# Graph attention with turned scores and a graph convolution with tiles of one bin each, in a new order of operations

## What is computed

```python
# graph attention (edges sorted by dst)
el = jnp.sum(feat_src_e * attn_l[edge_type], axis=-1)
er = jnp.sum(feat_dst_e * attn_r[edge_type], axis=-1)
e = jax.nn.leaky_relu(el + er, negative_slope=0.2)
m = jax.ops.segment_max(e, edge_dst, num_segments=N_NODES)
ex = jnp.exp(e - m[edge_dst])
denom = jax.ops.segment_sum(ex, edge_dst, num_segments=N_NODES)
h = jax.ops.segment_sum((ex / denom[edge_dst])[..., None] * feat_src_e, edge_dst, num_segments=N_NODES)
# graph convolution
filt = jax.nn.silu(rbf @ Wf1 + bf1) @ Wf2 + bf2
agg = jax.ops.segment_sum(x[col] * filt, row, num_segments=N_NODES)
```

## Time and profile before

| | |
|---|---|
| median of 3 runs | 4170.98 us (4170.66 to 4171.43) |
| the profiled execution | 4176.44 us |
| its span, first to last instruction | 4174.7 us |
| PE busy | 2928.3 us, 70% of the span |
| DVE busy | 2177.3 us, 52% |
| ACT busy | 1210.5 us, 29% |
| POOL busy | 2277.2 us, 55% |
| mean granted TensorE clock | 0.858 of full speed |

### The profile page before, as it was taken

One profiled execution on the slowest core, in us unless ns is written; L12 is line 12 of the kernel. 1 busy time (PEld: TensorE's weight loads), 2 busy tenths in 40 slices (PEclk: granted clock), 3 DMA queues, 4 the chain that ended last, 5 costly groups with the idle time before them and its releaser, 6 DMA issues. The chain is left out here.

```text
span 4174.7 us, 73619 instructions
## 1 busy us (share of the span) xinstructions
PE 2928.3 (70%) x20296; PEld 2364.7 (57%) x20297; DVE 2177.3 (52%) x5961; ACT 1210.5 (29%) x3266; POOL 2277.2 (55%) x2336
## 2 busy tenths in 40 slices
PE   5199101777777777776379679999999864299990
PEld 1188101555555555555255358888888633288990
DVE  8411002877777777777743557777777444011112
ACT  1123000444444444444223223333333231022220
POOL 2777775777777777777240056666666200511115
PEclk8599655998998999999679789999999875599995
DMA  3344101222222222225100143333335501155533
GB/s 105 108 135 137 40 2 32 63 65 63 63 64 63 64 64 63 64 64 62 23 19 1 47 136 89 90 89 90 90 90 84 52 0 39 49 175 173 171 104 114
DMA packets 209214, 317.71 MB, mean 76 GB/s; under 512 B 63367, under 2 KB 150063, under 8 KB 208388
## 3 DMA queue, kind: packets, MB, share of 16 engines
q0 software_dynamic: 95008, 179.89, 19.9%
q1 hardware_dynamic: 103204, 127.24, 9.4%
q10 hardware_dynamic: 10944, 9.97, 0.7%
HBM read 248.03 MB, written 68.84 MB: 76 GB/s over the span
## 5 line engine op out<-in xcount | busy, mean ns | idle before, releaser
L1402 POOL DMA_INDIRECT conv_got<-xtab,conv_rowidx x588 | 565.8, 962 | 313.2 <-DVE conv_msg L1507 156.6
L806 POOL DMA_INDIRECT att_got<-feat,att_rowidx x588 | 573.2, 975 | 201.5 <-issue 150.2
L294 POOL DMA_INDIRECT table<-l0a_rec,l0a_addr x469 | 458.2, 977 | 216.7 <-issue 146.1
L1454 PE MATMUL conv_pf<-conv_wf,conv_act 128*128 128x256 f32 x2352 | 534.0, 380 | 0.2 <-DVE conv_filt L1502 0.2
L812 POOL DMA_INDIRECT table<-recs_rec,recs_addr x432 | 423.2, 980 | 131.6 <-issue 130.4
L1454 PEld LDWEIGHTS conv_pf<-conv_wf,conv_act 128*128 128x128 f32 x2352 | 447.6, 190 | 76.9 <-issue 0.8
L982 PE MATMUL att_pmax<-all_identb,att_away 128*128 128x512 bf16 x588 | 261.1, 444 | 203.9 <-DVE att_elo L901 203.2
L863 DVE TENSOR_REDUCE att_tmax<-att_pmax 128x4 f32<-128x512 f32 x588 | 373.8, 680 | 31.1 <-PE att_pmax L986 27.6
L986 PE MATMUL att_pmax<-all_identb,att_ehi 128*128 128x128 bf16 x2352 | 383.6, 242 | 0.0
L986 PE MATMUL att_pmax<-all_identb,att_elo 128*128 128x128 bf16 x2352 | 383.3, 242 | 0.0
L1420 ACT ACTIVATE conv_act<-conv_p,conv_bf 128x512 f32<-128x512 f32 x294 | 186.2, 684 | 552.1 <-PE conv_p L1446 552.1
(11 more groups left out here) (336 smaller groups left out, 5074.0 us busy)
## 6 DMA issues: line engine op xcount, KB each, us to landing
moe_w<-in_L_ffn_w SPq DMA_DIRECT2D x96, 512.0 KB
feat<-proj_out SPq DMA_DIRECT2D x30, 1040.0 KB
results<-moe_y ACTq DMA_DIRECT2D x76, 128.0 KB, 1.7
att_got<-feat,att_rowidx POOLq DMA_INDIRECT x588
conv_got<-xtab,conv_rowidx POOLq DMA_INDIRECT x588, 2.8
xtab<-ln_row SPq DMA_DIRECT2D x60, 128.0 KB, 1.7
table<-l0a_rec,l0a_addr POOLq DMA_INDIRECT x469
table<-recs_rec,recs_addr POOLq DMA_INDIRECT x469, 2.1
```

Source lines behind the costliest of these rows:

```text
L294: self.nc.gpsimd.indirect_dma_start(out=self.table, out_offset=bass.IndirectOffsetOnAxis(ap=self.addrs[:, j:j + 1], axis=0), in_=self.recs ...
L806: nc.gpsimd.indirect_dma_start(out=got[g % 3][:, k, :], out_offset=None, in_=feat, in_offset=bass.IndirectOffsetOnAxis(ap=rowidx[:, g * K ...
L1402: nc.gpsimd.indirect_dma_start(out=got[g % 3][:, k, :], out_offset=None, in_=xtab, in_offset=bass.IndirectOffsetOnAxis(ap=rowidx[:, g * K ...
L1454: ins = nc.tensor.matmul(pf[b][:, k, :], act1[s3][:, h, (2 * b + k) * P:(2 * b + k + 1) * P], wf2[:, h, :], start=(h == 0), stop=(h == 1))
```

## The change

The convolution gets its own padding: `table1` is sorted into tiles of one bin each instead of groups of one bin, so it needs ET1 = 500 tiles, or 125 groups of four. The four tiles of a group can now belong to four bins: TensorE writes four sums, two to a bank, VectorE loads four bin numbers and makes four additions to `agg`, spread over the step between other work.

In attention the scores of a group are written as bf16 parts into `spread`, turned by TensorE (`pE`), copied by ScalarE (`eT`) and brought into `pmax` by one matmul of 512 columns a tile, which a constant `select` directs; so `pmax` takes eight matmuls of 512 columns a group. VectorE reduces all four banks in one instruction. ScalarE scales `acc` by `keep` (`shrunk`, four instructions), and VectorE adds `psum` in one. The pipeline has four slots and five stages (groups t to t-4), the kinds of all edges (`typ`) are computed once ahead of the loop, and the order in each engine's step is new: sums, products and additions of old groups stand early in a step, and small dependent instructions alternate with others.

The sends to `table1` are redistributed: 214 in attention (none for the first four groups, then one or two in turn), 12 beside `join_attention`, 26 beside the second layer norm, 24 beside the mixture's routing, 167 in the mixture and 26 beside the third layer norm. The numbers of all sends and of the gathers in attention stay.

The diff, cut; for the steps of `attend`, whose old form stands above, only the new side is shown.

```diff
 K = 4
 ET = 588
 TS = ET + -(-EJ // P)
+ET1 = 500
+TS1 = ET1 + -(-EJ // P)
+assert (EDGES + NT * (P - 1)) // P <= ET1 and ET1 % K == 0
 assert 0 < EV <= EJ and (EDGES + NT * (K * P - 1)) // (K * P) <= ET // K and ET % (3 * K) == 0
 COLS0 = 20, 44, EJ - 64
-ROUND = 3
-COLS1 = ROUND * (ET // K - 3), EJ - ROUND * (ET // K - 3)
-assert sum(COLS0) == EJ == sum(COLS1) and COLS1[1] > 0
+COLS1 = ET // K - 4 + (ET // K - 4) // 2, 12, 26, 24, 167, 26
+assert sum(COLS0) == EJ == sum(COLS1)
 RELS, HEADS, HD = 8, 4, 64
 FW = D + HEADS
 NG = 20
...
+            sends = [0 if g < SLOTS else 1 + g % 2 for g in range(GROUPS)]
+            assert sum(sends) == COLS1[0]
             for g in range(GROUPS):
+                u = g % SLOTS
                 if g >= SLOTS:
+                    pool.wait_ge(f_ready, g - SLOTS + 1)
+                    pool.wait_ge(last_ready, (g - SLOTS + 1) * LAST)
                 for k in range(K):
                     nc.gpsimd.indirect_dma_start(
...
+                wait_positive(pool, sent[u], 16 * sum(sends[u:g:SLOTS]))
+                for i in range(sum(sends[:g]), sum(sends[:g + 1])):
                     nc.gpsimd.indirect_dma_start(
                         out=table1, out_offset=bass.IndirectOffsetOnAxis(ap=addr1[:, i:i + 1], axis=0),
+                        in_=rec1[:, i, :], in_offset=None).then_inc(sent[u], 16)
+            for u in four:
+                pool.wait_ge(sent[u], 16 * sum(sends[u::SLOTS]))
...
+            v.memset(acc[:, :, :, :], 0.0).then_inc(ready, 1)
...
+            v.tensor_tensor(typ[:, :, :], bcast(c["ramp"][:, 0:RELS], [[0, ET], [1, RELS]]),
+                            recs[:, :, 2].unsqueeze(2).broadcast_to([P, ET, RELS]), ALU.is_equal).then_inc(ready, 1)
...
+                    at = [bcast(spread[s1][:, 0, q * K * HEADS:], [[HEADS, K], [ROWS + 1, HEADS]]) for q in range(2)]
+                    dve.wait_ge(er_ready, g1 + 1)
+                    v.tensor_tensor(ert[:, :, :, :], per[:, :, 0:RELS * HEADS].rearrange("p k (r h) -> p k h r", r=RELS),
+                                    typ[:, bass.ds(g1 * K, K), :].unsqueeze(2).broadcast_to([P, K, HEADS, RELS]), ALU.mult).then_inc(picked, 1)
+                    dve.wait_ge(picked, g1 + 1)
+                    v.tensor_reduce(ers[:, :, :], ert[:, :, :, :], AX.X, ALU.add).then_inc(ers_ready, 1)
                 if 0 in parts:
...
+                    wait_positive(dve, sum_ready, t - 3)
...
+                if 1 in parts:
+                    dve.wait_ge(got_s[s1], ((i + 1) if u else i) * 16 * K)
+                    dve.wait_ge(ers_ready, g1 + 1)
+                    v.tensor_tensor(z[:, :, :], ers[:, :, :], got[s1][:, :, D:FW], ALU.add).then_inc(z_ready, 1)
...
+                    dve.wait_ge(ex_ready, g3 + 1)
+                    wait_positive(dve, sum_ready, g3 - 1)
+                    n = ON_DVE
+                    v.tensor_tensor(f[(u - 3) % 2][:, 0:n, :, 0:HD], got[s3][:, 0:n, 0:D].rearrange("p k (h d) -> p k h d", h=HEADS),
+                                    ex[:, 0:n, :].unsqueeze(3).broadcast_to([P, n, HEADS, HD]), ALU.mult).then_inc(f_ready, 1)
+                if 4 in parts:
+                    bin4 = bin_of(dve, g4)
+                if 1 in parts:
+                    dve.wait_ge(z_ready, g1 + 1)
+                    v.scalar_tensor_tensor(out=e[s1][:, :, :], in0=z[:, :, :], scalar=SLOPE, in1=z[:, :, :], op0=ALU.mult, op1=ALU.max).then_inc(e_done, 1)
+                if 4 in parts:
+                    dve.wait_ge(sum_ready, g4 + 1)
...
+                    dve.wait_ge(sum_ready, g4 + 1)
+                    dve.wait_ge(shrunk_ready, (g4 + 1) * HEADS)
+                    v.tensor_tensor(flat(flat(acc[:, bass.ds(bin4, 1), :, :], "p a b c -> p a (b c)")), flat(shrunk[:, :, :]), psum[:, 0:HEADS * H1], ALU.add).then_inc(acc_done, 1)
+                if 1 in parts:
+                    dve.wait_ge(e_done, g1 + 1)
+                    wait_positive(dve, spread_turned, g1 - 3)
+                    v.tensor_copy(at[0], e[s1][:, :, :]).then_inc(high, 1)
...
+                    dve.wait_ge(max_ready, g2 + 1)
+                    v.tensor_reduce(tmax[:, :], pmax[:, :, :, :].rearrange("p k h e -> p h k e"), AX.XY, ALU.max).then_inc(tmax_ready, 1)
+                    bin2 = bin_of(dve, g2)
+                if 1 in parts:
+                    dve.wait_ge(high, g1 + 1)
+                    v.tensor_tensor(at[1], e[s1][:, :, :], at[0], ALU.subtract).then_inc(e_ready, 1)
+                if 2 in parts:
+                    m = flat(mrun[:, bass.ds(bin2, 1), :])
+                    dve.wait_ge(tmax_ready, g2 + 1)
+                    wait_positive(dve, m_kept, g2)
+                    v.tensor_tensor(mnew[:, :], tmax[:, :], m, ALU.max).then_inc(mnew_ready, 1)
+                    dve.wait_ge(mnew_ready, g2 + 1)
+                    wait_positive(dve, me_ready, g2)
+                    v.tensor_copy(mparts[:, 0, :], mnew[:, :]).then_inc(m_high, 1)
+                    dve.wait_ge(m_high, g2 + 1)
+                    v.tensor_tensor(mparts[:, 1, :], mnew[:, :], mparts[:, 0, :], ALU.subtract).then_inc(m_ready, 1)
+                    wait_positive(dve, keep_ready, g2)
+                    v.tensor_tensor(drop[:, :], m, mnew[:, :], ALU.subtract).then_inc(drop_ready, 1)
+                    dve.wait_ge(drop_ready, g2 + 1)
+                    v.tensor_scalar(m, mnew[:, :], 0.0, None, ALU.add).then_inc(m_kept, 1)
+                    dve.wait_ge(me_ready, g2 + 1)
+                    wait_positive(dve, col_ready, g2)
+                    v.tensor_tensor(below[:, :, :], e[s2][:, :, :], pme[:, :, 0:HEADS], ALU.subtract).then_inc(below_ready, 1)
...
+                if 3 in parts:
+                    g = t - 3
                     act.wait_ge(below_ready, g + 1)
                     wait_positive(act, f_ready, g)
                     wait_positive(act, last_ready, g * LAST)
                     nc.scalar.activation(ex[:, :, :], below[:, :, :], ACT.Exp).then_inc(ex_ready, 1)
+                    wait_positive(act, sum_ready, g - 1)
+                    nc.scalar.activation(f[(u - 3) % 2][:, :, :, HD], below[:, :, :], ACT.Exp).then_inc(col_ready, 1)
+                if 4 in parts:
+                    g = t - 4
+                    wait_positive(act, acc_done, g)
+                    act.wait_ge(keep_ready, g + 1)
+                    for h in range(HEADS):
+                        nc.scalar.activation(shrunk[:, h, :], flat(acc[:, bass.ds(bin4, 1), h, :]), ACT.Copy,
+                                             scale=keep[s4][:, h:h + 1]).then_inc(shrunk_ready, 1)
                 if 0 in parts:
                     act.wait_ge(oh_ready, t + 1)
+                    wait_positive(act, max_ready, t - 3)
+                    wait_positive(act, turned, t - 3)
                     nc.scalar.activation(away[u][:, :, :], oh[u][:, :, :], ACT.Identity, bias=c["minus_big"][:, 0:1], scale=BIG).then_inc(away_ready, 1)
...
+                    act.wait_ge(got_s[s3], ((i + 1) if u == 3 else i) * 16 * K)
+                    products(ON_DVE)
...
+                if 3 in parts:
+                    for k in range(ON_DVE + 1, K):
+                        products(k)
+                if 2 in parts:
+                    g = t - 2
+                    act.wait_ge(drop_ready, g + 1)
+                    wait_positive(act, shrunk_ready, (g - 3) * HEADS)
+                    nc.scalar.activation(keep[s2][:, :], drop[:, :], ACT.Exp).then_inc(keep_ready, 1)
+                if 1 in parts:
+                    g = t - 1
+                    act.wait_ge(spread_turned, g + 1)
+                    wait_positive(act, max_ready, g - 1)
+                    nc.scalar.activation(flat(eT[(u - 1) % 2][:, :, :]), pE[:, 0:HEADS * P], ACT.Copy).then_inc(eT_ready, 1)
...
+                def sums(g, ks):
+                    for k in ks:
+                        if k >= ON_DVE:
+                            pe.wait_ge(last_ready, g * LAST + (k - ON_DVE + 1) * HEADS)
+                        ins = nc.tensor.matmul(psum[:, 0:HEADS * H1], oh[s3][:, k, :], flat(f[(u - 3) % 2][:, k, :, :]), start=(k == 0), stop=(k == K - 1))
+                    return ins
...
+                if 3 in parts:
+                    g = t - 3
+                    wait_positive(pe, acc_done, g)
+                    pe.wait_ge(col_ready, g + 1)
+                    pe.wait_ge(f_ready, g + 1)
+                    sums(g, range(ON_DVE + 1))
                 if 0 in parts:
                     pe.wait_ge(ohT_ready, t + 1)
+                    wait_positive(pe, picked, t)
                     for k in range(K):
                         for n in range(3):
                             ins = nc.tensor.matmul(per[:, k, 0:RELS * HEADS], ohT[u][:, k, :], flat(erparts[:, n, bass.ds(bin0, 1), :]),
                                                    start=(n == 0), stop=(n == 2))
                     ins.then_inc(er_ready, 1)
+                if 1 in parts:
+                    g = t - 1
```

(56 more changed lines are left out.)

333 lines of the change are left out of this document (111 added, 222 removed).

## The result

The changed kernel takes 3886.3 us (median of 4 runs, 3884.7 to 3893.1); the kernel before took 4171.0 beside it. The ratio is 0.9321, 95% interval 0.9304 to 0.9337: 285 us less. The forecast was 3823, so 63 us of the expected gain are missing.

A forecast was written before the change was run, and what follows sets the result against it. GpSimd's DMA issue was taken to bound attention and TensorE the convolution; 258 - 15 in attention, -19 mixture, -1 layer norm, +122 and +3 convolution gave 348 us less, predicting 3823 us, range 3775 to 3950.

The forecast's parts named there:

- second rival: Convolution: VectorE becomes the bound, 6.2 to 6.6 us a step, 62 us more, total 3885; chance 0.10.
- Attention, GpSimd: Attention step: 5.5 DMAs on average at 1.273 us, a floor of 7.00 us; step taken as 7.15.
- Attention, chain: Attention: dependent work through all engines around single-buffered `pmax`, 6.0 to some 6.3 us at full clock, below 7.00.
- first rival: Attention: the cross-engine chain, not GpSimd, sets the step, 7.7 to 8.3 us; total 3900 to 3990; chance 0.16.
- Attention, ends: Attention's start: later first `f` from memset, `typ` and one more pipeline step, +15 us, bounds +8 and +20.
- Sends moved, the join: Join: 12 moved sends at 1.27, 15 us, lie inside its 27 us and so cost nothing.
- Layer norms and routing: Moved sends beside layer norms and routing are covered, except 0 to 3 us for one layer norm, taken 1.
- Mixture: Mixture: 167 sends take 212 us, so the stage becomes GpSimd's and ends 19 us later, bounds 17 and 22.
- Convolution: Convolution: TensorE stays the bound, 125 steps of 5.89 us, minus 122 us; VectorE 5.3 to 5.9 a step.
- (fourth): Attention: gathers, not GpSimd's issue, are slow; step stays at 8.9 us, only convolution gains, total 4080; chance 0.06.
- (third): Attention: TensorE at half clock throughout, step 10.8 us instead of 8.92, total 4355; chance 0.02.

The follow-up runs named there:

- best_b: Changed kernel plus join in pieces with 18 sends, 161 mixture sends, mixture bias added by VectorE in pieces, `acc` memset before the records wait; 3838.4 us, ratio 0.9204.

## Why the prediction was right, and where 63 us went

The direction, the size and the order of the parts held: 3886 lies in the range, and two thirds of what the two long loops gained came from attention and a third from the convolution, as worked out. But it lies just above the forecast's own bounds (3775 to 3880), and that it meets the second rival's 3885 is luck: that rival's mechanism held, but it gave 25 of the 63 us, and the rest comes from three other places.

**Attention, GpSimd.** Right in kind: the floor of 5.5 DMAs is the step. The term of 1.273 us a DMA was mis-sized: it is 1.315. 786 DMAs in 146 steps are 5.38 a step, 7.08 us, and with 0.22 of waits that is 7.30 for 7.15. 146 x 0.15 = 22 us. The 1.273 came from one group of a trace, but it was no lucky one: the mean over the old stage is 1.276. What changed is how many DMAs start beside VectorE's `f` and one-hots, one in five instead of one in nine, and how long they are held there (1.22 us in the mean instead of 1.04). That VectorE holds them is read from the trace and from the join; no run changed it in this stage.

**Attention, chain.** 6.0 to 6.3 us were forecast at full clock, 6.51 measured, because `pmax` has 0.32 us a matmul and not 0.22; the other links together are 0.3 to 0.5 us shorter than forecast. I had scaled a block's time by columns (0.66 x 1024/1536); eight matmuls of 512 columns take 2.56 us, nearly as long as the four old blocks together (2.64). It stayed below GpSimd at a clock of 0.93. At 0.71 it didn't: GpSimd waits a third of the time, and the first rival's mechanism holds, at a higher price (10.36 us) than its 7.7 to 8.3.

**Attention, ends.** +15 forecast, +13.8 measured. The memset and `typ` cost what was said (6.56 and 5.03 us), and best_b shows that 8.0 of it needn't be there.

**Sends moved, the join.** The step that failed: "12 x 1.27 = 15 lies inside the join's 27 us". I compared lengths and not what runs beside what. 24.5 us of the join are three VectorE instructions with both inputs in SBUF, and a send can't pass them. The trace of before had a sign, though with GpSimd's arithmetic and not with a send. In its mixture GpSimd adds a bias for 16.42 us from 2141.0, and beside it VectorE needs 16.32 us for 30 columns:

```profile
2141.13 16.32 DVE L1261 TENSOR_SCALAR mix_top<-mix_top 128x30 f32<-128x30 f32 x1 [10.77 <-ACT mix_top L1232]
```

The same work takes 0.18 us when GpSimd doesn't hold it (1932.28 after). Layer norms and routing, whose VectorE instructions are short, cost 1 us as forecast.

**Mixture.** GpSimd became its bound as forecast: VectorE is done 27.5 us before the next stage. +24 for +19: the sends took the 212 us, but from the last one's end (2161.2) it is 7.0 us to the next stage, where I had taken 2 for the landing. No run shows the 2: the join's end comes 3.4 us after its last send's.

**Convolution.** The step that failed: "TensorE stays the bound". VectorE's arithmetic was if anything too high (4.29 + 1.0 = 5.3, measured 4.8 without gaps). The register loads were too low: 0 to 0.6 us for three more, where four and the loop's turn cost 6.13 - 4.8 = 1.3 us and the three had 0.66 of it. So a step takes 6.13 (6.04 of it VectorE's own) against TensorE's 5.84. That is the second rival's mechanism at a smaller size than its 6.2 to 6.6, and it is 0.24 a step above the 5.89 taken: 30 us, of which 25 are missing after the better start. VectorE's steps of 6.44 lie where the loop turns; before, TensorE's bound hid that.

**The other rivals.** The gathers were not the limit (fourth): VectorE waits 71.1 us for them, 221.8 before. The half clock throughout (third) did not come: the granted clock of attention is 0.93 for 0.92, and even in the groups at the lower clock it is 0.71. By the Trainium skill, "TensorE: Matmul & The Clock Gate", section "HAM oscillation", bursts parted by waits for data run at the low clock again and again; the trace agrees that it falls again and again (to half 27 times in this loop, 56 times in the old one), and not that it stays there: it is at half for 153 of the 1065.5 us.

## What to carry to other kernels

Work that is to be hidden beside other work must be held against what runs there, instruction by instruction: a DMA that GpSimd issues waits for a long VectorE instruction with both inputs in SBUF, and cutting that instruction into pieces of 0.6 us gave 10 us back here. A register load on VectorE keeps the next instruction 0.8 to 1.0 us behind the start of the one ahead (one-hot to addition 0.78, `filt` to addition 0.99), so each load wants a long instruction of its own that doesn't wait, and none wants to stand behind another. A price taken from the old trace, even its mean, holds only for what ran beside it there: the DMA's rose from 1.276 to 1.315 us when fewer of them shared a step with the same VectorE work.
